# Masks of all 32 tiles loaded by two DMAs in the setup, in place of two small DMAs a tile

## The reference, cut to what matters

```python
scores = jnp.einsum('bhqd,bhkd->bhqk', q, k) / jnp.sqrt(jnp.float32(HDIM))   # 16 heads of 16
causal = kj <= qi + 1
scores = jnp.where(causal[None, None], scores, jnp.float32(MASK_OUT))
zero_col = jnp.zeros(attention_mask.shape[:-1] + (1,), attention_mask.dtype)
mask = jnp.concatenate([zero_col, attention_mask], axis=-1)                   # (64, 1, 1, 65)
scores = scores + mask
attn = jax.nn.softmax(scores, axis=-1)
out = jnp.einsum('bhqk,bhkd->bhqd', attn, v)
...
x = x + linear_attention_and_layernorm(out @ c_proj_w + c_proj_b)
x = x + ffn(lstm(x))
```

## Time and profile before

| | us |
|---|---|
| median of 3 runs | 1017.58 |
| the three runs | 1018.38, 1017.58, 1013.61 |
| profiled execution | 1014.53 |
| its span, first to last instruction | 1012.4 |
| busy PE / DVE / ACT / POOL | 866.5 / 805.1 / 495.7 / 346.8 |

### The profile page before, as it was taken

One profiled execution on the slowest core, in us unless ns is written; L12 is line 12 of the kernel. 1 busy time (PEld: TensorE's weight loads), 2 busy tenths in 40 slices (PEclk: granted clock), 3 DMA queues, 4 the chain that ended last, 5 costly groups with the idle time before them and its releaser, 6 DMA issues.

```text
span 1012.4 us, 27497 instructions
## 1 busy us (share of the span) xinstructions
PE 866.5 (86%) x9798; PEld 579.3 (57%) x9798; DVE 805.1 (80%) x2157; ACT 495.7 (49%) x1177; POOL 346.8 (34%) x436
## 2 busy tenths in 40 slices
PE   3359887988989898988977899999999999999984
PEld 1246655666666666666654565565665665666642
DVE  6388999778777877788764688888888888888884
ACT  2264656666676667666653333433343433333431
POOL 0053667555555556555642011111111111111111
PEclk9588999999999999999999999999999999999997
DMA  4600011011001110111010000000000000000001
GB/s 108 197 13 21 19 37 33 22 36 34 27 24 34 34 31 20 34 34 33 17 31 17 1 12 21 22 21 21 17 17 21 21 22 21 19 14 22 21 22 26
DMA packets 41239, 30.36 MB, mean 30 GB/s; under 512 B 12082, under 2 KB 40050, under 8 KB 41173
## 3 DMA queue, kind: packets, MB, share of 16 engines
q1 hardware_dynamic: 41172, 29.42, 10.3%
HBM read 20.87 MB, written 8.54 MB: 29 GB/s over the span
## 4 chain that ended last, share of the span: by engine, by line
PE 39%; DVE 23%; issue 13%; ACT 5%; POOL 2%; DVEq 1%; POOLq 0%; ACTq 0%
PE bank L713 14%; PE bank L882 8%; PE bank L981 6%; PE bank L871 6%; DVE hqT L1533 3%; PE bank L973 3%; ACT hqT L1183 2%; DVE kv_bd L1381 2%; DVE pT L458 2%; ACT qk L1054 1%; DVE h_value L170 1%; DVE qk L1375 1%; PE bank L718 1%; DVE prob L1323 1%; DVE v L1394 1%
## 5 line engine op out<-in xcount | busy, mean ns | idle before, releaser
L665 POOL TENSOR_TENSOR ffn_room<-h_value,h_scale 128x704 f32<-128x704 f32 x32 | 44.4, 1388 | 291.7 <-DVE h_value L171 291.7
L713 PE MATMUL bank<-gu,xqT 128*128 128x512 f16 (+1 forms) x576 | 128.2, 362 | 1.3 <-DVE xqT L1548 1.3
L613 POOL TENSOR_TENSOR p<-prob,p 128x520 f16<-128x520 f32 x64 | 80.5, 1258 | 68.4 <-ACT p L1065 68.3
L882 PE MATMUL bank<-wh,h 128*64 128x512 f16 x768 | 100.2, 385 | 3.5 <-ACT h L1158 2.1
L871 PE MATMUL bank<-wx,x1T 128*64 128x512 f16 x768 | 93.8, 379 | 0.9 <-DVE x1T L441 0.9
L772 PE MATMUL bank<-ident,p 128*65 128x128 f16 x1024 | 76.0, 223 | 16.5 <-ACT qT L1119 9.9
L981 PE MATMUL bank<-dn,hqT 128*128 128x256 f16 x576 | 70.3, 278 | 20.7 <-DVE hqT L1533 20.7
L1148 ACT ACTIVATE sig<-bank 128x256 f32<-128x256 f32 x64 | 24.8, 388 | 127.2 <-PE bank L882 126.6
L871 PEld LDWEIGHTS bank<-wx,x1T 128*64 128x64 f16 x768 | 78.9, 202 | 11.2 <-DVE x1T L441 1.2
L713 PEld LDWEIGHTS bank<-gu,xqT 128*128 128x128 f16 x576 | 53.7, 98 | 53.6 <-issue 9.9
L606 POOL TENSOR_TENSOR prob<-prob,row_max 128x520 f32<-128x520 f32 x64 | 68.5, 1089 | 37.0 <-DVE row_max L1331 36.8
(11 more groups left out here) (199 smaller groups left out, 2064.0 us busy)
## 6 DMA issues: line engine op xcount, KB each, us to landing
x_in<-in_x_columns SPq DMA_DIRECT2D x32, 128.0 KB, 2.2
x_res<-in_x SPq DMA_DIRECT2D x32, 128.0 KB, 2.1
x_rows<-x_rows_sb SPq DMA_DIRECT2D x32, 128.0 KB, 1.9
ffn_room<-x_rows SPq DMA_DIRECT2D x64, 64.0 KB, 2.2
out<-ffn_room SPq DMA_DIRECT2D x64, 64.0 KB, 2.0
mask_in<-in_mask_Bx1x1xS_ff SPq DMA_DIRECT2D x64, 16.0 KB, 2.4
x1T<-in_L_cond_Wx SPq DMA_DIRECT2D x1, 1024.0 KB, 6.5
x1T<-in_L_cond_Wh SPq DMA_DIRECT2D x1, 1024.0 KB, 8.5
```

Source lines behind the costliest of these rows:

```text
L613: pool.tensor_tensor(p16[:, 1, r, :], prob[:, r, :], p16[:, 0, r, :], ALU.subtract).then_inc(s["p_lo"], 1)
L665: pool.tensor_tensor(blocks(hq, FF), blocks(fp4_h.value, FF), spread(fp4_h.scale, FF), ALU.mult).then_inc(s["hq_ready"], 1)
L713: last = pe.matmul(dst, lhs(a, c), rhs(b, c), start=first and c == 0 and a == b, stop=c == C - 1 and (a, b) == parts3[-1], skip_group_chec ...
L882: last = pe.matmul(bank[e][B * h:B * h + B, :], h16[:, m, c, :], half_cols(wh16, a, c, h), start=False, stop=True, skip_group_check=True)
```

## The change

The two mask loads of a step go. In the setup, right behind the bias rows and ahead of step 0's `x_in` load, SP issues two DMAs: each loads the masks of all 32 tiles for one half of the partitions (32 rows of 256 bytes, from every second row in DRAM, to each of 64 partitions). `mask_in` grows from 512 bytes to 8 KB a partition. DVE waits for the two loads once, in step 0; SP no longer waits for `mask_ready`. The mask sum's source is picked by the tile's number, which in the loop is a register value, where it was picked by the parity.

```diff
-    mask_rows = mask.rearrange("b u v s -> b (u v s)")
+    mask_sides = mask.rearrange("(n e) u v s -> e n (u v s)", e=2)
...
-    mask_in = sb("mask_in", [P, 2, S])
+    mask_in = sb("mask_in", [P, NT, S])
...
-    mask_loaded = [sem(f"mask_loaded{i}") for i in range(2)]
+    mask_loaded = sem("mask_loaded")
...
+        for b in range(2):
+            sp.dma_start(mask_in[64 * b:64 * b + 64, :, :], mask_sides[b].partition_broadcast(S)).then_inc(mask_loaded, 16)
+
         def late_loads():
...
-                after(sp, s["mask_ready"], t1.count(back=2))
-                for b in range(2):
-                    row = mask_rows[t1.number() * 2 + b]
-                    sp.dma_start(mask_in[64 * b:64 * b + 64, q, :], row.partition_broadcast(S)).then_inc(mask_loaded[q], 16)
...
             if t1:
-                dve.wait_ge(mask_loaded[t1.parity], mask_count(t1))
+                if t1.loop is None and t1.b == 0:
+                    dve.wait_ge(mask_loaded, 16 * 2)
                 after(dve, s["masked"], t1.count(2, 2, back=1))
-                dve.scalar_tensor_tensor(out=add_mask[:, 0:S], in0=mask_in[:, t1.parity, :], scalar=SCORE,
+                dve.scalar_tensor_tensor(out=add_mask[:, 0:S], in0=mask_in[:, t1.number(), :], scalar=SCORE,
                                          in1=causal[:, 0:S], op0=ALU.mult, op1=ALU.add).then_inc(s["mask_ready"], 1)
```

## The result

The changed kernel is slower: 1022.12 us, median of 10 runs (1018.50 to 1023.27), against 1017.77 us, median of 10 (1013.61 to 1020.06). The ratio is 1.0049, 95% interval 1.0035 to 1.0064, so +5.0 us, between 3.6 and 6.5. The forecast was 1018.3 us in a range of 1013 to 1024, no change within 0.5%, with +2.3 us as the sum. The side and the place were right; the size was half.

What follows compares the result with a forecast made beforehand. It took the loop as bound by the tile's own cycle, through DVE, and the start by a serial chain through SP. Known executions' average 1016.0 + 2.3 (start) + 0 (loop) = 1018.3 us, range 1013 to 1024.

Steps and rivals of the forecast that it cites:

- The place: Start, SP's queue: bulk loads ahead of the image store delay it, w_down, Wx and all that follows by 2.3 us.
- The loop at 0: Loop: removed loads, dropped waits and the register address together change nothing; bounds -0.65 to +1.7 us, taken as 0.
- rival C: Loop, DVE: the register address shows, 1.7 us, with the start's 2.3 together 1020.0 us; chance 0.12.
- Rival D: Loop: each removed small load had cost its 2.4 us latency, 74 us over 31 tiles, about 944 us; chance 0.02.
- rival B: Start: masks move at 404 GB/s, 2.6 us, shift -0.6; 0.65 us gained from DVE's sequencer; 1014.8 us; chance 0.13.
- The transfer: Start: the two bulk loads, 1.049 MB, take 5.5 us, between bounds of 4.6 and 8.6 us.
- The slack: Start: the part of the transfer that delays nobody, 3.2 us; the shift is the transfer time less this.
- Rival A: Start: transfer much slower than its bytes say, slower by over 0.5%; 1021.4 us at the upper bound; chance 0.20.

Runs made afterwards that it cites:

- e1: The kernel before, loop unchanged, plus the two bulk mask loads in the setup into a buffer nobody reads: 1021.30 us, ratio 1.0059.
- e2: The changed kernel with masks of tiles 0 and 1 loaded after x_in, the rest behind the late weight loads: 1016.35 us, ratio 1.0007 to before.
- e5: The changed kernel with the two bulk loads issued once more, right behind the first, into an unread buffer: 1027.63 us, ratio 1.0108 to before.
- e10: The kernel before plus an unread bulk load, 256-byte pieces from their own places in x, one DMA on 128 partitions: 1020.05 us, ratio 1.0034.
- e4: The kernel before plus two unread bulk loads on 64 partitions each, 8 KB runs from a shared source: 1019.69 us, ratio 1.0054.
- e6: The kernel before plus two unread bulk loads on 64 partitions each, 8 KB runs, each partition its own source: 1019.66 us, ratio 1.0026.
- e9: The kernel before plus one unread bulk DMA on 128 partitions, 8 KB runs, each partition its own source: 1017.59 us, ratio 1.0004.
- e3: The kernel before plus two unread bulk loads on 64 partitions each, 256-byte pieces from their own places in x: 1022.34 us, ratio 1.0077.
- e8: The changed kernel with the two bulk mask loads issued before SP's wait for the bias stores: 1021.94 us, ratio 1.0054 to before.

## Why the prediction was right and where it wasn't

**The place: right, shown.** The loss is in the start, through the image store, `w_down` and `Wx`, as forecast; e1 has it without the changed loop, e2 has the changed loop without it, e5 issues the transfer twice and pays the second one in full.

**The loop at 0: right.** 300.70 and 300.80 us for 21 tiles. The register instruction (rival C) is there, 65 to 82 ns, 20 times:

```profile
L1401 DVEq FUSED_REGOPS  x20: 65/74/82, 206.4 to 478.5; - x20
```

but the mask sum still starts 0.77 us behind the first `v` subtraction, as before:

```profile
322.25 0.85 DVE L1393 TENSOR_TENSOR v<-bank,v 64x256 f16<-64x256 f32 x2
323.02 0.21 DVE L1401 SCALAR_TENSOR_TENSOR add_mask<-mask_in,causal 128x64 f32<-128x64 f32 x1
```

The wait that left took register work (line 1399 before, 53 ns every second tile) and a semaphore instruction of 21 ns with it; neither gave anything that can be seen. Rival D, the latency of each small load, is out: nobody waited, and e2 against before shows no gain. So is rival B, a hidden transfer at 404 GB/s: it went at 170, and the start moved by +4.4 and not by -0.6 us.

**The transfer: mis-sized.** Forecast 5.5 us, measured 6.4 (e5). The step that failed is the scaling of a sparse rate to a share of 1: it gave 227 GB/s as the lower bound's rate, and 170 were measured. The pieces' records in a full queue are 33 ns long and not 18, and the share doesn't end at 1. Part of that is that each DMA writes 64 partitions: in e10, on 128, it is 1.38 x 16 x 2 us for 1719 pieces, 26 ns each. I had taken the value near the lower bound; the upper one, 8.6 us from the `gamma` and `beta` loads, was above the truth and its reasoning (a shared source) wrong.

**The slack: mis-sized.** Forecast 3.2 us, measured 2.0. It let the masks' data begin 4.2 us after the first bias-row load (28.4 less 24.2), and it began after 4.8 (28.0 less 23.24). And it gave `x_in` and the image store 1.6 us from the end of the masks to the landing; from 34.2 to 36.5 it was 2.3, as the queue moved 149 GB/s in the last window above. That makes 1.3 us, against 1.2 by e5. Both errors, of transfer and slack, have one sign; with 0.9 and 1.2 us they are the 2.1 us between +2.3 and +4.4. So the forecast was right in its place and its side, but that the result stayed within 0.5% was close: 0.49% was measured, with an interval from 0.35 to 0.64%.

**Rival A** (over 0.5%) had 0.20; at 0.49% the result lies on its border, and its deciding point, a transfer of 8.3 us, should have been 7.1. Its chance was too low, since both bounds of the transfer already lay on the side of a loss.

**Open.** e4's ratio (+3.4 to +7.3 parts in a thousand) is above what its start of 2.6 us gives; its profiled execution was its fastest. The clock's scatter would cover it, but that isn't shown. Why the clock falls in some executions at the change of phase and not in others isn't known either.

## What to carry to other kernels

Sixty-four small loads that nobody waits for cost nothing, and one large load costs its length, less the slack, if it is put ahead of something on the start's serial chain: look at who waits for what stands behind it in the queue, not at the number of issues. Size a bulk load from a stretch in which the queue is full, and count the partitions it writes: two DMAs of 64 partitions were slower than one of 128 with the same bytes. Where the start is a chain of landings, issue first what the first tile waits for first; here that gave 6 us, more than the 5 us that the change lost.

## What the runs showed of the hardware that I had not expected

- DMAs that write 64 partitions in runs of 8 KB moved 232 to 243 GB/s over 3 us, with a shared source and with their own (e4, e6); one that writes 128 partitions moved 352 GB/s over 3 us and 410 at its best (e9). With pieces of 256 bytes it is 162 against 220 GB/s (e3, e10).
- Many partitions reading one small source isn't slower than each reading its own: 160 GB/s in e1, 162 in e3.
- The DMA share of a window reached 1.39 (changed kernel, e1, e3): the records of an engine's pieces overlap. Scaling a sparse rate to a share of 1 gave 227 GB/s where 170 were measured.
- Two issues of 2048 pieces each held SP for 2.1 us behind the bias rows (changed kernel) and for 12.7 us while what stood ahead in the queue moved 7 to 30 GB/s (e8).
- The ten executions of the changed kernel differ by almost 5 us, with a mean granted clock of 0.964 at the fast end and 0.956 at the slow one.
